# A three-layer cross-feature kernel: one more chunk's right-hand fields loaded instead of picked on TensorE, and both products of loaded chunks kept in PSUM with both low parts on VectorE

## The reference, cut to what matters

```python
X0 = inputs.reshape(64, 32, 64)                     # batch b, field h, embedding d
Xi, pools = X0, []
for W, b in ((W1, b1), (W2, b2), (W3, b3)):         # each makes 128 units
    Wr = W.reshape(128, 32, m)                      # m = 32, then 128, 128
    Xi = jnp.einsum('bhd,bmd,ohm->bod', X0, Xi, Wr) + b[None, :, None]
    pools.append(Xi.sum(axis=-1))                   # over d
y = jnp.concatenate(pools, axis=-1) @ fc_W.T + fc_b # (64, 1)
```

## Time and profile before

| | us |
|---|---|
| median of 3 runs | 80.14 (80.0 to 80.24) |
| the profiled execution's own time | 80.34 |
| its span in the trace | 78.5 |
| PE busy | 73.3 (93%) |
| PEld / DVE / ACT / POOL busy | 52.4 / 47.3 / 34.6 / 49.5 |

### The profile page before, as it was taken

How to read it: one execution, slowest core, us unless ns; L and a number is a source line. 1 busy time by engine, 2 the same in 40 slices (tenths; PEclk the granted TensorE clock), 3 DMA queues, 4 the chain that set the end, 5 groups by cost and what they waited for, 6 DMA issues and landing times.

```text
span 78.5 us, 1146 instructions
## 1 busy us (share of the span) xinstructions
PE 73.3 (93%) x372; PEld 52.4 (67%) x372; DVE 47.3 (60%) x45; ACT 34.6 (44%) x51; POOL 49.5 (63%) x48
## 2 busy tenths in 40 slices
PE   3999699997899999999999999999999999999970
PEld 1326178674448277878888888888888888886840
DVE  1056999989939849467759864799922300303541
ACT  1833897917594689754909245205800003000000
POOL 4987969999039519990583997796199970062300
PEclk9999999999999999999999999999999999999999
DMA  1899999999975435271499960000000000000000
GB/s 16 260 326 287 400 360 349 353 385 389 385 232 147 128 102 165 68 193 34 89 405 370 385 267 0 8 0 4 0 0 0 0 0 0 8 0 0 0 0 0
DMA packets 7529, 12.01 MB, mean 153 GB/s; under 512 B 835, under 2 KB 3971, under 8 KB 7267
## 3 DMA queue, kind: packets, MB, share of 16 engines
q1 hardware_dynamic: 6915, 11.16, 42.2%
q10 hardware_dynamic: 608, 0.77, 3.0%
HBM read 10.88 MB, written 1.05 MB: 152 GB/s over the span
## 4 chain that ended last, share of the span: by engine, by line
PE 82%; DMA 7%; POOL 3%; DVE 3%; issue 1%; SPq 1%; DVEq 0%; POOLq 0%
PE a_ps L591 28%; PE x_ps L591 28%; DMA w_sb<-w 7%; PE z_ps L585 7%; PE a_ps L684 5%; PE x_ps L619 3%; PE a_ps L657 3%; PE a_ps L646 2%; PE a_ps L645 2%; POOL w_sb L306 2%; POOL z_lo L310 2%; DVE w_hi L496 2%; PE a_ps L671 1%; PE x_ps L770 1%; PE a_ps L672 1%
## 5 line engine op out<-in xcount | busy, mean ns | idle before, releaser
L267 POOL TENSOR_TENSOR feat<-r_in,feat 128x1024 fp32r<-128x1024 f32 x8 | 19.6, 2448 | 6.4 <-ACT feat L358 6.1
L591 PE MATMUL x_ps<-feat,w_hi 128*128 128x512 f32 x64 | 18.8, 393 | 0.0
L591 PE MATMUL a_ps<-feat,a_hi 128*128 128x512 f32 x64 | 16.3, 396 | 0.0
L260 POOL TENSOR_TENSOR xs<-x_in,xs 32x512 fp32r<-32x512 f32 x7 | 10.0, 1428 | 8.3 <-ACT xs L358 8.0
L508 DVE SCALAR_TENSOR_TENSOR x<-a_ps,vec,x 128x512 f32<-128x512 f32 x7 | 5.2, 749 | 14.5 <-PE a_ps L646 14.5
L591 PEld LDWEIGHTS x_ps<-feat,w_hi 128*128 128x128 f32 x64 | 12.1, 188 | 2.7
L591 PEld LDWEIGHTS a_ps<-feat,a_hi 128*128 128x128 f32 x64 | 11.9, 188 | 2.7
L274 POOL TENSOR_TENSOR x<-x 128x512 f32<-128x512 f32 x6 | 7.8, 1294 | 6.7 <-DVE x L508 6.3
L358 ACT ACTIVATE feat<-z_ps 128x1024 fp32r<-128x1024 f32 x8 | 8.2, 1027 | 7.6 <-DVE z_ps L475 7.6
L475 DVE TENSOR_TENSOR z_ps<-x_in,z_ps 128x1024 f32<-128x1024 f32 x6 | 7.4, 1230 | 5.3 <-PE z_ps L585 5.2
L358 ACT ACTIVATE feat<-r_in 128x1024 fp32r<-128x1024 f32 x8 | 8.4, 1055 | 3.7 <-DVE r_in L475 3.7
(11 more groups left out here) (76 smaller groups left out, 75.6 us busy)
## 6 DMA issues: line engine op xcount, KB each, us to landing
w_sb<-w SPq DMA_DIRECT2D x9, 512.0 KB, 8.8
x_in<-xl SPq DMA_DIRECT2D x8, 256.0 KB, 6.3
r_in<-xr SPq DMA_DIRECT2D x2, 1024.0 KB, 6.4
a_by_fields<-at_sb SPq DMA_DIRECT2D x8, 96.0 KB, 2.0
x<-x ACTq DMA_DIRECT2D x1, 512.0 KB, 4.6
x<-x SPq DMA_DIRECT2D x1, 512.0 KB, 6.0
w_sb<-w SPq DMA_DIRECT2D x1, 256.0 KB, 6.3
a_by_fields<-at_sb SPq DMA_DIRECT2D x4, 64.0 KB, 1.8
```

The lines of the kernel that those rows point to most:

```text
L260: nc.gpsimd.tensor_tensor(xs[rows, c, :], x_in[rows, c % X_BUFS, :], xs[rows, c, :].bitcast(f32), ALU.subtract).then_inc(xs_lo, 1)
L267: nc.gpsimd.tensor_tensor(feat[:, c, 1, of_half(1), :], z_of(c, 1), feat[:, c, 0, of_half(1), :].bitcast(f32), ALU.subtract).then_inc(lo_d ...
L591: nc.tensor.matmul(bank, weights[:, k, :], feat[:, c, part, k, :], start=(start and k == 0), stop=False)
```

## The change

PICKED goes from 6 to 5. Chunk 5's right fields are loaded (DMA issued right after `load_x(5)`, 1 MB into buffer 0 of `r_in`), and its four picking matmuls go. Loaded chunks (5, 6, 7) use the two buffers of `r_in` in turn and keep the products of both halves in the two bank pairs of `z_ps`; `second_lo` makes half 1's low part on VectorE, counted by a new semaphore `late_lo`. Picked chunks put half 1's product where its low part will stand (`prods[c]`), so `r_in` is free from the start. `lo(5)`, `lo(6)` and `lo(7)` leave GpSimd's list; `product(2)` comes after all of chunk 7; on ScalarE a small copy (`v_rep`) and `save_x1(2)`, `save_x1(3)` come earlier in the list.

```diff
-PICKED = 6
+PICKED = 5
...
+        for c in range(PICKED):
+            places.enter_context(nc.sbuf_tensor(f"other_parts_of_{c}", [P, 3 * PER_HALF * N], f32))
+            prods.append(places.enter_context(nc.sbuf_tensor(f"products_of_{c}", [P, PER_HALF, N], f32)))
...
+        def right_buf(c):
+            return (c - PICKED) % 2
         def z_of(c, half):
-            if half == 0:
-                return field_bank(c, 0)
-            if c < PICKED:
-                return r_in[:, 1, of_half(c % 2), :]
-            return r_in[:, c % 2, of_half(1), :]
+            if half == 0 or c >= PICKED:
+                return field_bank(c, half)
+            return prods[c][:, :, :]
...
             def load_right(c):
-                if c % 2 == 0:
+                if c == PICKED:
                     sp.wait_ge(spread_done, 3)
-                else:
-                    sp.wait_ge(hi_done, count(PICKED - 1, 1))
-                    sp.wait_ge(lo_done[1], PICKED)
-                sp.dma_start(r_in[:, c % 2, :, :], xr[c]).then_inc(r_here[c % 2], 16)
+                if c >= PICKED + 2:
+                    sp.wait_ge(z_done, count(c - 2, 1))
+                sp.dma_start(r_in[:, right_buf(c), :, :], xr[c]).then_inc(r_here[right_buf(c)], 16)
...
             load_x(5)
+            load_right(PICKED)
             load_x(6)
...
-            load_right(PICKED)
+            load_right(PICKED + 1)
...
-            load_right(PICKED + 1)
+            load_right(PICKED + 2)
...
             lo(4)
-            lo(5)
...
-            lo(6)
...
-            lo(7)
...
             hi(4, 1)
+            save_x1(2)
             act.wait_ge(zeros_done, ZEROS)
             act.wait_ge(a_out, A_OUT)
...
-            save_x1(2)
             hi(5, 0)
+            save_x1(3)
             hi(5, 1)
...
-            save_x1(3)
...
+            def second_lo(c):
+                features_free(dve, c)
+                dve.wait_ge(z_done, count(c, 1))
+                dve.wait_ge(hi_done, count(c, 1))
+                nc.vector.tensor_tensor(feat[:, c, 1, of_half(1), :], z_of(c, 1),
+                                        feat[:, c, 0, of_half(1), :].bitcast(f32), ALU.subtract).then_inc(late_lo, 1)
             def chunk(c):
                 mult(c, 0)
                 mult(c, 1)
                 lo(c)
+                if c >= PICKED:
+                    second_lo(c)
...
             lo(6)
+            second_lo(6)
             mult(7, 0)
             mult(7, 1)
+            lo(7)
+            second_lo(7)
             product(2)
-            lo(7)
...
             x1_hi(3, 0)
-            pick_right(5, 0)
             x1_tail(2)
             x1_lo(3, 0)
             x1_hi(3, 1)
-            pick_right(5, 1)
             x1_lo(3, 1)
```

More of the change, by code:

```diff
@@ L80, in cin_kernel @@
         blank = at_sb[:, 1, :].bitcast(mybir.dt.bfloat16)
+        places, prods = ExitStack(), []
+        for c in range(PICKED):
+            places.enter_context(nc.sbuf_tensor(f"other_parts_of_{c}", [P, 3 * PER_HALF * N], f32))
+            prods.append(places.enter_context(nc.sbuf_tensor(f"products_of_{c}", [P, PER_HALF, N], f32)))
+        places.close()
         feat = sb("feat", [P, CHUNKS, 2, TILES, N], f32r)
@@ L122, in cin_kernel @@
         xs_hi, xs_lo, picked = sem("xs_hi"), sem("xs_lo"), sem("picked")
-        z_done, hi_done = sem("z_done"), sem("hi_done")
+        z_done, hi_done, late_lo = sem("z_done"), sem("hi_done"), sem("late_lo")
         lo_done = [sem("lo_done_a"), sem("lo_done_b")]
@@ L331, in _ @@
             lo(4)
-            lo(5)
-            pool.wait_ge(lo_done[1], 6)
+            pool.wait_ge(lo_done[1], PICKED)
             split_x(6)
@@ L345, in _ @@
                 left, steps = left // 2, steps + 1
-            lo(6)
             pool.wait_ge(xsum_done, 4)
-            pool.wait_ge(lo_done[1], 7)
+            pool.wait_ge(xs_lo, 7)
             split_x(7)
             pool.wait_ge(xs_lo, CHUNKS)
-            lo(7)
             for c in range(1, CHUNKS - 1):
@@ L419, in _ @@
             save_x1(1)
+            act.wait_ge(v_saved, 1)
+            copy(v_rep[:, :, :], v_st[:, 0:H].rearrange("o (h r) -> o h r", r=1).to_broadcast(
+                [P, H, 4])).then_inc(v_saved, 1)
             save_a(2)
@@ L432, in _ @@
                     scratch.tensor, (TILES * j + k) * M, [[(EXT + 1) * M, H], [1, (TILES - k) * M]])).then_inc(f_main_in, 16)
-            save_x1(2)
             hi(5, 0)
+            save_x1(3)
             hi(5, 1)
-            act.wait_ge(v_saved, 1)
-            copy(v_rep[:, :, :], v_st[:, 0:H].rearrange("o (h r) -> o h r", r=1).to_broadcast(
-                [P, H, 4])).then_inc(v_saved, 1)
-            save_x1(3)
             act.wait_ge(f_sum, 1)
@@ L464, in mult @@
                     right = field_bank(c, half)
-                    if half == 1 and c >= 2:
-                        dve.wait_ge(hi_done, count(c - 2, 1))
-                        dve.wait_ge(lo_done[1], c - 1)
-                else:
-                    dve.wait_ge(r_here[c % 2], 16)
-                    right = r_in[:, c % 2, tiles, :]
+                    if half == 1:
+                        features_free(dve, c)
+                else:
+                    dve.wait_ge(r_here[right_buf(c)], 16 * ((c - PICKED) // 2 + 1))
+                    right = r_in[:, right_buf(c), tiles, :]
                     if half == 0:
                         dve.wait_ge(z_done, count(c - 1, 1))
-                        dve.wait_ge(lo_done[0], c - 1)
+                        dve.wait_ge(lo_done[0], c)
+                    elif c == PICKED:
+                        dve.wait_ge(lo_done[0], c)
+                    if half == 0 and c > PICKED:
+                        dve.wait_ge(late_lo, c - PICKED)
                 left = x_in[:, c % X_BUFS, :].rearrange("p (k n) -> p k n", k=1).to_broadcast([P, PER_HALF, N])
@@ L609, in x1_hi, with low_parts @@
                 x1_low_weights(c, half)
+            def low_parts(c, half):
+                if half == 1 and c >= PICKED:
+                    pe.wait_ge(late_lo, c - PICKED + 1)
+                else:
+                    pe.wait_ge(lo_done[half], c + 1)
             def x1_lo(c, half):
-                pe.wait_ge(lo_done[half], c + 1)
+                low_parts(c, half)
                 terms(x1_ps[c % 2][:, :], c, half, w1_hi, 1)
```

## The result

| | before | after |
|---|---|---|
| median, us | 80.19 (80.0 to 80.4, 4 runs) | 79.17 (79.06 to 79.46, 4 runs) |
| profiled execution, us | 80.34 | 79.46 |
| its span, us | 78.5 | 77.7 |

The ratio is 0.9883 with a 95% interval of 0.9863 to 0.9903: faster by 1.2%. A second set of runs gave 79.25 beside 80.12 (0.9892, 0.9876 to 0.9909). The forecast was 79.3, that is 0.83 us less; the medians moved by 1.02 us in the first set and by 0.87 us in the second.

What follows compares the result with a forecast made beforehand. PE was taken to bound the kernel, dense from 20 to 75 us with 82% of the chain; -0.93 us (picking) + 0.1 (a_hi) = -0.83, giving 79.51 profiled and 79.3 median, range 79.0 to 79.9.

Steps and rivals of the forecast that it cites:

- Four matmuls, 0.93 us: On PE: chunk 5's four picking matmuls go, 0.46 and 0.47 us, so PE is 0.93 us earlier from 35.2 us on.
- the last eight: PE's timeline: from 20 us on, no row has idle time before it until the last eight matmuls.
- The load costs nothing: Chunk 5's 1.05 MB load, issued near 15 us, takes 2.8 us of queue; price 0, bound from above 0.3 us.
- The cover: Chunk 5's load lands near 24 or 25 us, some 7 us before a mult could use it.
- GpSimd's low part of chunk 5 would have been late: Left on GpSimd, it ends at 41.03 but PE wants it at 40.58: half the gain would be a wait.
- Chunk 5's mults and GpSimd block each other: Mults from r_in and GpSimd's low parts take turns; second mult ends at 37.8, without blocking 34.8.
- GpSimd's low part of chunk 4: On GpSimd: ends at 36.6, wanted by PE at about 37.2, so it holds.
- a_hi, 0.1 us: The a_hi copy ends at 41.5, PE wants it at 41.41; costs 0.1 us, upper bound 0.5 us.
- My 2 us to spare for the rest of A: The rest of f1 and f2, landing at 40.12 before its add, is wanted at 44.3: 2 us to spare, price 0.
- product(2), 0: Behind all of chunk 7, it ends at 56.9 to 57.4, wanted by a_product(4) at 57.38; cost 0, bound 2.5 us.
- where I had 0.3 us and dropped it: GpSimd's split and gather around 49 to 51.6 can block chunk 7's first mult by 0.3 us; taken as 0.
- The sum: -0.93 + 0.1 = -0.83 us: profiled execution 80.34 to 79.51, span 77.7, median 79.31.

Runs made afterwards that it cites:

- the dead load: Kernel before plus a 1 MB load nobody uses, issued right behind chunk 5's left fields: 80.11 us; upper level 80.12 beside 80.09.
- the next profile: Kernel after, unchanged, run and profiled once more beside more runs of the kernel before: 79.25 us, before 80.12.
- low parts left on GpSimd: Kernel after, but low parts of chunks 5 to 7's second halves stay on GpSimd, their products in SBUF, product(2) at its old place: 80.16 us.
- GpSimd held back: Kernel after, with GpSimd's low part of chunk 4 waiting until both mults of chunk 5 are done: 79.42 us.
- chunk 4 loaded: Kernel after with subtraction first and product(2) ahead of chunk 7's low parts, plus chunk 4's right fields loaded (PICKED 4): 77.91 us.
- both edits alone: Kernel after with product(2) ahead of chunk 7's low parts and GpSimd's low part of chunk 1 behind VectorE's small subtraction: 78.04 us.

## Why the prediction was right, by its own steps

1. **Four matmuls, 0.93 us.** Right: 0.97 between the profiles, all of it given back when four matmuls returned. (The first row of PE with idle time behind 20 us is that of the last sixteen matmuls, at 75.65, not of the last eight.)
2. **The load costs nothing.** Right for one load, by the dead load. I had it land near 24 or 25 us; it landed at 27.0, as it stood behind left fields that landed at 24.0 themselves in the profile of before. The cover was 5 us and not 7. The experiments added the limit: 2 MB ahead of the stores put the loads of f1 and f2 off by 1.8 us.
3. **GpSimd's low part of chunk 5 would have been late.** Right in kind, too small in size: I had half the gain as a wait; left in place it takes the whole gain, 1.02 us.
4. **Chunk 5's mults and GpSimd block each other.** Right in kind. I had the second mult end at 37.8, that is 37.5 with the 0.27 us by which this execution was ahead; it ended at 37.12. The Trainium skill's rule (page "SBUF — State Buffer", section "Who interferes with whom") names this contention; the trace agrees: 4.94 us with GpSimd's reads beside them, 2.74 without most of them. GpSimd's low part of chunk 4 had more room than I wrote: I had it wanted at about 37.2, but its matmuls stand at 38.54 in the timeline of before, so they would be at 37.61 after the change.
5. **a_hi, 0.1 us.** Mis-sized: 0. The a_hi copy began at 40.17 where I had 40.8 (40.5 with the offset), and PE did not wait at 41.10. My 2 us to spare for the rest of A were counted to the wrong matmul: VectorE adds the rest of f ahead of the low part of A, and PE wants that low part about 1 us sooner. It ended at 41.59 and was used at 43.02. With 2 MB loaded this was a wait.
6. **product(2), 0.** Mis-sized the other way in the profiled execution. I had it end between 56.9 and 57.4 (the steps that I listed add up to 56.7) and wanted at 57.38; with the offset of 0.27 us, between 56.6 and 57.1 and wanted at 57.1. It ended at 57.32, and the fifth A product began 0.30 us late (57.36, its usual step would give 57.06). Product(1) was not late (47.90), so the time was lost behind it: 0.37 us in chunk 7's mults beside the gather, where I had 0.3 us and dropped it, and about 0.4 us between the mults and `product(2)`, where the last low part stands behind lo(7) (54.29 to 55.52), which my sum left out. In the next profile the mults took 2.37 us and the loss was 0. A step taken at nothing while its own sum ended between half a microsecond of cover and none should have carried part of that.
7. **The sum.** 79.51 for the profiled execution, measured 79.46: -0.27 (start) - 0.97 (picking) + 0.30 (fifth A product) + 0.09 (its eight matmuls with a_hi took 1.95 us from start to start behind the wait, 1.86 before) makes -0.85, for 0.88 measured. Without the early start, which has nothing to do with the change, it would have been near 79.7: that this total agreed so closely is luck. 79.31 for the median against 79.17 and 79.25 is the fairer measure, and there the second profile shows the mechanism without the loss.

What I did not see at all: that the kernel before has two levels 1.1 us apart, more than the change is worth. What I take for the cause stood in the profile of before, in the same shape as the pair that I did use: a small subtraction of 2.48 us at 17.37 on VectorE while GpSimd's low part ran from 17.18, and PE waiting 0.81 us behind it.

## What to carry to other kernels

In a stretch where PE is dense, a matmul taken off is worth its step (0.23 us here), but only if the work that fed the next matmuls was ahead by more; write down for each input when it ends and when it is wanted, since several of them here came only 0.5 us or less ahead. An engine that is dense with reads next to another can turn a 0.5 us instruction into a 2.5 us one; look for instructions whose duration is not that of their shape, and decide their order with a semaphore when a matmul waits for one. The best kernel of these runs with a narrow spread has the change, GpSimd's low part of chunk 1 behind the small subtraction, and product(2) ahead of chunk 7's low parts: 78.04 us, 2.6% under the 80.11 of before in the same set. About half of that is the order of the subtraction, which the kernel before can have as well (79.09).

## What the runs showed of the hardware that I had not expected

- A small instruction can wait for a large one: 32 rows x 256 on VectorE took 2.48 us beside a GpSimd operation of 2.38 us, and 0.42 us when it came first. GpSimd's operation began only 0.07 to 0.24 us ahead, and one program on one core had two times, 80.1 and 79.0 (that this race makes them is inferred, see above).
- A wait costs PE more than its idle time: the two matmuls behind one took 0.57 to 0.58 us from start to start instead of 0.45 (low parts left on GpSimd, GpSimd held back, chunk 4 loaded).
- With 1 MB more issued at 15 us, A's stores, issued from 23 us on, took 2.2 and 2.3 us to land instead of 2.0 and 1.8. With 2 MB they took 4.8 and 4.5 us (2.7 with both edits alone, that is with 1 MB), and the loads that wait for them were issued 1.8 us later.
